# One low part of six on POOL instead of two, and a layer norm threaded into the attention that follows it

## The reference

```python
# the end of layer 2: out is the experts' mixture
out = _layer_norm(out + x, gamma, beta)                # "l3"; then t = t + out gives x4
# layer 3, attention on a = _ln_t(t)                   # "a4"
q, k, v = rmsnorm(a, w_norm1) @ w_qkv                  # "n4", then k4, v4, q4
q = elu(q) + 1; k = elu(k) + 1
kv = einsum('bnhd,bnhm->bhdm', k, v)                   # "kv4"
z = 1 / (einsum('bnhd,bhd->bnh', q, k.sum(1)) + 1e-6)  # "den4", "z4"
out = einsum('bnhd,bhdm,bnh->bnhm', q, kv, z)          # "num4", "o4"
h = a + out @ w_out + b_out; t = t + h + rmsnorm(h, w_norm2)
# layer 3, experts on flat = _ln_t(t)                  # "a5"
probs = softmax(flat @ router_w.T)                     # two best of 8 a token
h = silu(flat @ w1[e].T) * (flat @ w3[e].T)            # hidden width 682
out = sum over the two experts of gate * (h @ w2[e].T)
```

## Time and profile before

| | us |
|---|---|
| median of 3 runs (lowest, highest) | 1118.35 (1116.3, 1120.89) |
| the profiled execution | 1117.59 |
| its span, first to last instruction | 1115.7 |
| PE, DVE, ACT, POOL busy | 906.7, 807.1, 693.3, 706.2 |
| mean granted TensorE clock | 0.925 of full |

### The profile page before, as it was taken

How to read it: one execution, slowest core, us unless ns; L and a number is a source line. 1 busy time by engine, 2 the same in 40 slices (tenths; PEclk the granted TensorE clock), 3 DMA queues, 4 the chain that set the end, 5 groups by cost and what they waited for, 6 DMA issues and landing times.

```text
span 1115.7 us, 21247 instructions
## 1 busy us (share of the span) xinstructions
PE 906.7 (81%) x6566; PEld 512.5 (46%) x6566; DVE 807.1 (72%) x1661; ACT 693.3 (62%) x1287; POOL 706.2 (63%) x792
## 2 busy tenths in 40 slices
PE   4959999978999997788788764009999999999970
PEld 3435555533445752444454542005555555555540
DVE  7976666758875856788478887107888888888875
ACT  1845555545447546557566652008889889888875
POOL 2955555542778634577027777764888888888880
PEclk9979999998999998899899996559999999999995
DMA  5000000010003210002000000110111111111106
GB/s 222 1 2 1 2 1 1 1 48 24 1 1 102 64 40 0 1 2 69 21 7 24 26 26 30 60 31 22 32 36 32 32 36 32 31 37 31 32 23 229
DMA packets 25664, 39.59 MB, mean 35 GB/s; under 512 B 6420, under 2 KB 14488, under 8 KB 25304
## 3 DMA queue, kind: packets, MB, share of 16 engines
q1 hardware_dynamic: 16472, 28.86, 8.0%
q0 software_dynamic: 9088, 9.39, 2.8%
HBM read 24.76 MB, written 13.47 MB: 34 GB/s over the span
## 4 chain that ended last, share of the span: by engine, by line
PE 36%; POOL 34%; issue 14%; DVE 10%; ACT 4%; DMA 2%; POOLq 0%; SPq 0%; ACTq 0%; DVEq 0%
POOL results L769 13%; POOL slots L746 11%; POOL stage L781 7%; PE bank L1795 6%; PE bank L1806 3%; PE bank L1797 2%; PE bank L1872 2%; PE bank L1820 2%; POOL stage L728 1%; DVE T L854 1%; PE bank L1889 1%; PE bank L1823 1%; PE bank L2042 1%; PE bank L2067 1%; PE bank L1914 1%
## 5 line engine op out<-in xcount | busy, mean ns | idle before, releaser
L2285 PE MATMUL bank<-stage,big 128*128 128x512 f16 (+1 forms) x858 | 225.5, 382 | 9.5 <-issue 3.9
L1400 DVE TENSOR_TENSOR T<-bank,T 128x512 f32<-128x512 f32 x195 | 134.3, 689 | 95.1 <-ACT T L1713 90.8
L769 POOL DMA_INDIRECT results<-stage,small x156 | 171.5, 1100 | 37.6 <-issue 35.8
L746 POOL DMA_INDIRECT slots<-T,index x128 | 126.9, 991 | 85.1 <-DVE index L1310 46.9
L1713 ACT ACTIVATE T<-bank 128x512 f32<-128x512 f32 x234 | 139.5, 596 | 36.6 <-PE bank L2285 31.3
L1695 ACT ACTIVATE stage<-T 128x512 f16<-128x512 f32 x234 | 146.4, 626 | 1.3 <-DVE T L1402 0.4
L2261 PEld LDWEIGHTS bank<-l2w,stage 128*128 128x128 f16 (+1 forms) x1716 | 108.8, 98 | 79.7 <-issue 48.2
L2261 PE MATMUL bank<-l2w,stage 128*128 (+1 forms) x1716 | 134.6, 219 | 7.9 <-POOL stage L781 2.1
L781 POOL TENSOR_TENSOR stage<-T,stage 128x512 f16<-128x512 f32 x78 | 90.0, 1154 | 30.5 <-ACT stage L1695 27.7
L2285 PEld LDWEIGHTS bank<-stage,big 128*128 (+1 forms) x858 | 77.8, 101 | 63.6 <-issue 22.6
L1472 ACT ACTIVATE stage<-stage 128x512 f32<-128x512 f32 x64 | 40.3, 630 | 79.5 <-DVE stage L879 79.5
(11 more groups left out here) (379 smaller groups left out, 2023.2 us busy)
## 6 DMA issues: line engine op xcount, KB each, us to landing
stage<-slots SPq DMA_DIRECT2D x39, 130.0 KB, 2.0
stage<-in_w3l SPq DMA_DIRECT2D x8, 373.0 KB, 3.1
stage<-in_w1l SPq DMA_DIRECT2D x8, 320.0 KB, 2.9
results<-stage,small POOLq DMA_INDIRECT x156, 2.2
T<-in_xw SPq DMA_DIRECT2D x4, 512.0 KB, 5.9
X<-in_xi SPq DMA_DIRECT2D x1, 2048.0 KB, 14.7
slots<-T,index POOLq DMA_INDIRECT x128, 2.2
X<-results SPq DMA_DIRECT2D x8, 256.0 KB, 5.5
```

Source lines behind the costliest of these rows:

```text
L746: pool.indirect_dma_start(slots_d, bass.IndirectOffsetOnAxis(ap=index[:, k, n:n + 1], axis=0), rows5[:, n * RW:(n + 1) * RW], None).then_i ...
L769: pool.indirect_dma_start(results_d, bass.IndirectOffsetOnAxis(ap=IDS[t % 4][:, i:i + 1], axis=0), Y5[t % 2][:, i, :], None).then_inc(S(f" ...
L1400: nc.vector.tensor_tensor(H5[q], bank[3 + q][:, :], S5[q], ALU.mult).then_inc(S("hid5"), 1)
L2285: mm = nc.tensor.matmul(to[0:m, :], big16[:, bass.ds(e * UPW + o, m)], XT[s], start=(v % 2 == 0), stop=(v % 2 == 1))
```

## The change

Two independent parts.

Chunk 7's Ln and Exp come ahead of the Square of h4 (the last row). The diff, cut to its core:

```diff
+L3_CENTRED = [2, 3, 7, 4, 3, 4, 7, 7]
+L3_VARIANCE = [6, 5, 6, 5, 6, 5, 6, 6]
...
-        POOL_LOW = (1, 4)
+        POOL_LOW = (1,)
...
                 if t < NT:
                     low5_pool(t, POOL_LOW[0])
                 if t >= 1:
-                    results5(t - 1, (0, 1))
-                if t < NT:
-                    low5_pool(t, POOL_LOW[1])
-                if t >= 1:
-                    results5(t - 1, (2, 3))
+                    results5(t - 1, range(SUB))
...
@ DVE
-            for c in range(NCH):
+            def l3_vector(c):
                 dve.wait_ge(*when("l3_rstd", c + 1))
...
+            l3_vector(0)
+            l3_vector(1)
             nc.vector.tensor_copy(before16, mat("before")).then_inc(S("counting"), 1)
...
-            for k in range(NCH + 3):
+            l3_vector(2)
+            l3_vector(3)
+            a4_vector(0)
+            l3_vector(4)
+            n4_vector(0)
+            for k in range(1, NCH + 3):
...
                     k4_elu(k - 1)
+                if k in (1, 2):
+                    l3_vector(5 if k == 1 else 7)
...
                     n4_vector(k)
+                if k == 1:
+                    l3_vector(6)
...
@ ACT
-            ln_scalar(act, "l3", "eps5")
+            act.preload_act_table_set("natural_log_exp_and_others")
...
-            act.preload_act_table_set("natural_log_exp_and_others")
-            for k in range(NCH + 3):
+            l3_squared(0)
+            l3_squared(1)
+            l3_rooted(0)
+            l3_squared(2)
+            l3_rooted(1)
+            l3_squared(3)
+            l3_rooted(2)
+            squared("a4_sq", "a4_cen", 0, bank[0][:, :])
+            l3_squared(4)
+            l3_rooted(3)
+            logged("a4_ln", "a4_var", 0, bank[1][:, :], "eps5")
+            rooted("a4_rstd", "a4_ln", 0)
+            l3_rooted(4)
+            squared("n4_sq", "a4", 0, ch(A, 0))
...
                     k4_exp(k - 1)
+                if k in (1, 2):
+                    l3_rooted(5 if k == 1 else 7)
...
                     rooted("n4_rstd", "n4_ln", k)
+                if k == 1:
+                    l3_rooted(6)
                 if within(k - 1):
                     q4_exp(k - 1)
...
@ PE
+            def l3_centre(c):
+                pe.wait_ge(*when("y3_kept", 2 * (c + 1) if c < 3 else HALF))
+                held = [i for i in range(c) if L3_CENTRED[i] == L3_CENTRED[c]]
+                if held:
+                    pe.wait_ge(*when("l3", held[-1] + 1))
...
-                pe.wait_ge(*when("l3", min(NCH, c + 5)))
                 if c:
+                    pe.wait_ge(*when("l3", min(NCH, c + 2)))
...
                 if within(k):
                     a4_centre(k)
+                if k in (1, 2):
+                    l3_centre(5 if k == 1 else 7)
...
+                if k in (1, 2):
+                    l3_varied(5 if k == 1 else 7)
                 if within(k - 1):
                     v4_projected(k - 1)
+                if k == 1:
+                    l3_centre(6)
...
                     mean4("n4_ms", "n4_sq", k, bank[1][:, :])
+                if k == 1:
+                    l3_varied(6)
```

More of the change, by code:

```diff
@@ L1596, in _, with l3_squared, l3_rooted @@
             steps2(act, image_scalar, 0)
-            ln_scalar(act, "l3", "eps5")
+            act.preload_act_table_set("natural_log_exp_and_others")
+            def l3_squared(c):
+                act.wait_ge(*when("l3_cen", c + 1))
+                nc.scalar.activation(ch(T2, c), bank[L3_CENTRED[c]][:, :], ACT.Square).then_inc(S("l3_sq"), 1)
+            def l3_rooted(c):
+                act.wait_ge(*when("l3_var", c + 1))
+                nc.scalar.activation(ch(T2, c), bank[L3_VARIANCE[c]][:, :], ACT.Ln, bias=vec("eps5")) \
+                    .then_inc(S("l3_ln"), 1)
+                act.wait_ge(*when("l3_ln", c + 1))
+                nc.scalar.activation(ch(T2, c), ch(T2, c), ACT.Exp, scale=-0.5).then_inc(S("l3_rstd"), 1)
             def squared(op, ready, c, src):
@@ L1648, in within @@
                 return 0 <= c < NCH
-            act.preload_act_table_set("natural_log_exp_and_others")
-            for k in range(NCH + 3):
+            l3_squared(0)
[12 more added lines that the diff above has]
+            squared("n4_sq", "a4", 0, ch(A, 0))
+            logged("n4_ln", "n4_ms", 0, bank[1][:, :], "eps6")
+            rooted("n4_rstd", "n4_ln", 0)
+            for k in range(1, NCH + 3):
                 if within(k):
                     squared("a4_sq", "a4_cen", k, bank[0][:, :])
+                if k in (1, 2):
+                    l3_squared(5 if k == 1 else 7)
                 if within(k - 3):
@@ L2081, in _, with l3_varied @@
                 before3, chosen = chosen, next3
-            ln_tensor(pe, "l3", T1, "y3_kept", lambda c: 2 * (c + 1), left=HALF)
+            def l3_centre(c):
[3 more added lines that the diff above has]
+                    pe.wait_ge(*when("l3", held[-1] + 1))
+                nc.tensor.matmul(bank[L3_CENTRED[c]][:, :], mat("centre"), ch(T1, c), start=True, stop=True) \
+                    .then_inc(S("l3_cen"), 1)
+            def l3_varied(c):
+                pe.wait_ge(*when("l3_sq", c + 1))
+                if c >= 2:
+                    pe.wait_ge(*when("l3_ln", c if c == NCH - 1 else c - 1))
+                else:
+                    pe.wait_ge(*when("y3_kept", HALF))
+                nc.tensor.matmul(bank[L3_VARIANCE[c]][:, :], mat("mean"), ch(T2, c), start=True, stop=True) \
+                    .then_inc(S("l3_var"), 1)
             def mean4(op, ready, c, out):
@@ L2118, in v4_projected @@
                     pe.wait_ge(*chunk("q4_elu", c - 1))
+                else:
+                    pe.wait_ge(*when("l3", 5))
                 projected4("v4_proj", bank[3], c, "wv4")
@@ L2143, in den4_summed @@
                     pe.wait_ge(*chunk("h4", c - 1))
+                else:
+                    pe.wait_ge(*when("l3", 6))
                 attended4("den4", KSR, bank[4], c)
@@ L2148, in num4_summed @@
                     pe.wait_ge(*chunk("m4_ln", c - 1))
+                else:
+                    pe.wait_ge(*when("l3_ln", 6))
                 attended4("num4", KVR, bank[5], c)
@@ L2163, in a5_variance @@
                     pe.wait_ge(*chunk("pos5", c - 1))
+                else:
+                    pe.wait_ge(*when("l3", NCH))
                 mean4("a5_var", "a5_sq", c, bank[7][:, :])
@@ L2200, in within @@
                 return 0 <= c < NCH
-            for k in range(NCH + 3):
+            l3_centre(0)
+            l3_centre(1)
+            l3_varied(0)
+            l3_centre(2)
+            l3_varied(1)
+            l3_centre(3)
+            l3_varied(2)
+            a4_centre(0)
+            l3_centre(4)
+            l3_varied(3)
+            a4_variance(0)
+            l3_varied(4)
+            mean4("n4_ms", "n4_sq", 0, bank[1][:, :])
+            for k in range(1, NCH + 3):
                 if within(k):
                     a4_centre(k)
+                if k in (1, 2):
+                    l3_centre(5 if k == 1 else 7)
                 if within(k - 3):
```

13 lines of the change are left out of this document (8 added, 5 removed).

## The result

| | before | after |
|---|---|---|
| median, us (lowest, highest) | 1117.74 (1116.3, 1120.89) | 1105.64 (1104.08, 1107.1) |
| the profiled execution | 1117.59 | 1105.0 |
| its span | 1115.7 | 1103.1 |

Four runs of each. The ratio is 0.9891, 95% interval 0.9875 to 0.9907: 12.1 us faster, for a forecast of 14.8. The time fell inside the range. The two parts of the change did not share in it as forecast.

A forecast was written before the change was run, and what follows sets the result against it. Bounds: POOL's sends and low parts in the expert loop, and the late first send before it. Gains 11.8 + 1.3 + 1.7 = 14.8 us off 1117.59 gave 1102.8, median 1103.5; range 1098 to 1113.

The forecast's parts named there:

- The tile: Expert loop: moving low(4) to DVE cuts a tile from 8.33 to 8.02 us, 11.8 us in all.
- the ring: Expert loop: cycle of waits through POOL's low parts and sends; opened by low(4) on DVE, leaving 8.02 us a tile.
- The legs: Expert tile: up(2) to down(1) 3.56 us, on to next up(0) 1.84, back to up(2) 2.62.
- The register load: Expert loop, every second tile: PE's 0.33 us load becomes hidden; rival that it stays, 5.3 for 11.8 us, chance 0.25.
- The meeting of low parts: Expert loop: DVE's low part meeting a POOL instruction that reads SBUF costs 0.48 us; taken as zero in the sum.
- the slower rival: Expert loop: DVE becomes the bound through meetings with POOL; two a tile make 8.66 us, total 1127.9; chance 0.05.
- The tail: End of the expert loop: DVE does the last low parts, so the last sends finish earlier, 1.3 us.
- The norm: Last layer's start: interleaved norm chunks start chunk 0's a4 7.2 us earlier, of which the first send gets 1.7.
- the other end of the term (-1.3): Last layer: clock falls again while PE waits for bank 7, slot 2 costs some 3 us more, giving -1.3 for 1.7.
- The 1.3 for ACT: Last layer, slot 2: ACT does chunk 7's Ln and Exp ahead of the Square, taking 1.3 us of the gain.
- the 3.1 left: Last layer, slot 2: den4 starts at 546.6 for 549.71, so 3.1 us of the earlier start remain there.
- POOL's idle time: Expert loop: POOL was to idle over 1 us in each tile as a sign of the opened ring.

The follow-up runs named there:

- e3: Changed kernel with block 1's low part moved to DVE too, none left on POOL; ratio 0.992 to the kernel before, 1107.13 us.
- e8: Changed kernel with PE's register load in every tile instead of every second; ratio 0.9896 to the kernel before, 1105.48 us.
- e10: Kernel before with PE's register load in every tile instead of every second; ratio 1.0046 to the kernel before, 1124.07 us.
- e4: Kernel before with PE's register load one block later, behind down(5); ratio 0.9988 to the kernel before, 1115.16 us.
- e6: Changed kernel with chunk 7's two norm banks swapped and its Ln, Exp and DVE work at slot 2's end; ratio 0.9872, 1103.49 us.
- e9: Changed kernel with the next tile's turn on PE, and ACT's copy of it, issued earlier, ahead of down(1); ratio 0.9914, 1109.49 us.
- e2: Changed kernel with the experts' part undone, leaving the norm's part alone; ratio 0.9994 to the kernel before, 1116.68 us.

## Why the prediction was right, and where not

- *The tile.* Right in kind. Low(4) on DVE opened the ring, low(1) of POOL comes every 8.09 us, 8.05 and 8.13 in the two parities, and DVE no longer waits ahead of the first product. 8.02 was forecast; 38 x (8.36 - 8.09) = 10.3 us for 11.8. The legs miss by 0.08 us, most of it ahead of up(0); the tile before was 8.36 by its 38 steps, not 8.33, which made up for 0.03. What the account left out is how near the other rows stand: DVE's total of 7.7 us was put "below 8.02" and set aside, but with what lies between its instructions it is 7.8, and 8.13 with one low part more (e3).
- *The register load.* Taken as hidden, by inference; e8 and e10 show it, from both sides. The premise, that a wait just ahead makes it dear, is not the whole of it: e4's load costs 0.16 us where nothing just ahead waits.
- *The meeting of low parts,* the slower rival. It did not come: DVE's low parts take 0.692 us in the mean beside POOL's one a tile, as before, and 0.682 in e3 with none on POOL. The Trainium skill (SBUF — State Buffer, "Who interferes with whom") has the losing engine blocked fully; these rows leave 0.01 us a low part for it, since the two low parts hardly stand at the same time. The rule itself is not contradicted.
- *The tail.* 1.3 forecast, 1.2 measured.
- *The norm.* This step failed. It was to give 1.7. I took the clock as falling once and kept the second fall for the other end of the term (-1.3). It fell, as the granted clock of 0.53 shows, and the profile gave -0.6. Against the first multiplication the step had den4 at 30.6 us and the first send at 61.0; measured were 32.0 and 63.2. About 0.75 of den4's 1.4 is PE's centre for chunk 7, which started later than worked out, 29.6 us for 28.9 (n4's multiplication of chunk 1 started 0.5 late, and from there to the centre the working has 1.3 us, where its own 2 x 0.75 make 1.5 and 1.55 were measured), and 0.7 its two matmul groups at the low clock. Behind den4 another 0.8 is missing, since den4 and num4 took 1.07 us longer at that clock. The 1.3 for ACT was right (e6); less it, the 3.1 left are 1.8, which the working rounds to 1.7. That the bank would make PE wait was foreseen, and so was the second fall as a bound; what failed is to count on the clock staying full through that wait: in all six profiles with the wait for bank 7 it fell. Five profiles with this order have the first send at 61.8 to 63.2, mean 62.4, four with the old order at 62.6 to 63.2, mean 63.0. So the part's worth is nearer +0.6 than -0.6, and too small for the runs.
- *The numbers that fitted.* The first send was forecast at 577 and came at 577.5, den4 at 546.6 and came at 546.3. Neither confirms the step: 1.7 us of each come from the earlier start of the whole stage. Likewise the total of the spans, 12.6 for 14.8, misses by 2.2 us only because that start made up for part of 1.5 (tiles), 0.1 (tail) and 2.3 (norm).
- *POOL's idle time.* Over 1 us a tile was forecast; by its groups it is 47.3/31 = 1.5, only 0.4 of it ahead of low(1).

## What to carry to other kernels

Before an instruction is moved ahead on an in-order engine, ask of every buffer it needs who frees it and when: chunk 7's centre, which only waited for a bank, cost all that the interleaving of the norm won, and a swap of two bank numbers brought 5 us back. When a ring is opened, write down the full row of every engine in it, small waits included: DVE's row stood 0.3 us under the new tile, and both further cuts in the ring (e3, e9) loaded another row by as much as they freed, or more. And compare profiles from a mark just ahead of the changed code; absolute times agreed here with a forecast whose step was wrong.

## What the runs showed that I had not expected

- PE's short idle times cost twice. After 4.59, 3.06 and (in e6) 2.84 us of idle time the granted clock stood at 0.50 to 0.53; with four matmuls' worth of filler and 1.07 us of idle time left it stayed full (n4_ms 1.13 us for 2.08).
- The clock's return after the first fall varies from run to run with the same program in this stretch: the fourth matmul group behind n4_ms's start took 1.41 and 1.48 us in the changed kernel and e2, but 1.10 in e3, e8 and e9, whose first sends come 1.1 to 1.4 us earlier.
- A result send on POOL takes 0.95 to 1.46 us by its place. In e3, where DVE makes all six low parts around them, and in e9, with POOL's low part there, the mean is 0.98; in the changed kernel it is 1.23. The number of DVE's low parts is thus not the cause. What is stays open; in e3 and e9 the shorter sends brought no shorter tile.
